# Four layers of cross attention and experts on one core: where the experts' downward sums are added up in six of ten passes

## The reference, cut to what matters

```python
mixed = jnp.zeros((T, D))
for e in range(E):                                   # E = 8
    mixed = mixed + flat_cw[:, e:e + 1] * _swiglu(flat_z, w1[e], w3[e], w2[e])
```

## Time and profile before

| what | value |
|---|---|
| median of three runs | 4637.65 us |
| the profiled execution's own time | 4653.02 us |
| its span, from first to last instruction | 4651.2 us |
| outside the span | 1.8 us |
| mean granted TensorE clock | 0.958 of full speed |
| busy TensorE / ScalarE / VectorE / GpSimd | 3977.9 / 3939.7 / 2817.9 / 830.5 us |

### The profile page before, as it was taken

One profiled execution on the slowest core, in us unless ns is written; L12 is line 12 of the kernel. 1 busy time (PEld: TensorE's weight loads), 2 busy tenths in 40 slices (PEclk: granted clock), 3 DMA queues, 4 the chain that ended last, 5 costly groups with the idle time before them and its releaser, 6 DMA issues. The chain is left out here.

```text
span 4651.2 us, 69670 instructions
## 1 busy us (share of the span) xinstructions
PE 3977.9 (86%) x26742; PEld 905.9 (19%) x26742; DVE 2817.9 (61%) x5645; ACT 3939.7 (85%) x4355; POOL 830.5 (18%) x719
## 2 busy tenths in 40 slices
PE   6888888888789888888989999888888888888887
PEld 2121111111122211122212222111111111122112
DVE  4878888778777788867501110110486668876833
ACT  3589998899888889888898889978988888888994
POOL 4010001520025200352412111111000210035002
PEclk7699999999999999999999999999999999999998
DMA  4221001100011100111102121110001100010001
GB/s 123 63 63 30 12 14 32 34 12 13 15 52 35 44 24 19 32 32 35 32 17 70 44 68 31 34 39 17 15 12 37 35 11 12 12 38 27 9 1 48
DMA packets 124358, 150.38 MB, mean 32 GB/s; under 512 B 29208, under 2 KB 76320, under 8 KB 124016
## 3 DMA queue, kind: packets, MB, share of 16 engines
q1 hardware_dynamic: 122576, 145.05, 11.6%
q10 hardware_dynamic: 1440, 0.79, 0.1%
HBM read 122.24 MB, written 23.51 MB: 31 GB/s over the span
## 5 line engine op out<-in xcount | busy, mean ns | idle before, releaser
L956 ACT ACTIVATE prob<-scores 128x1024 f32<-128x1024 f32 x3264 | 3177.7, 1025 | 314.2 <-PE scores L787 299.6
L1070 DVE TENSOR_REDUCE mpart<-side 128x1 f32<-128x512 f32 (+1 forms) x3456 | 2124.2, 657 | 729.8 <-PE side L818 719.1
L797 PE MATMUL av<-prob,VA 128*9 128x512 f32 x6528 | 875.0, 609 | 1.7 <-ACT prob L956 0.8
L797 PE MATMUL av<-prob,VB 128*9 128x512 f32 x6528 | 874.0, 608 | 1.3 <-ACT prob L956 0.5
L787 PE MATMUL scores<-QP,KA 32*128 32x512 f16 x3264 | 641.9, 395 | 195.1 <-ACT above L964 118.3
L787 PE MATMUL scores<-QP,KB 32*128 32x512 f16 x3264 | 631.3, 388 | 191.3 <-ACT above L964 93.7
L818 PE MATMUL side<-KA,QP 32*128 32x512 f16 (+1 forms) x2112 | 625.1, 392 | 39.6 <-DVE mpart L1070 20.7
L818 PE MATMUL side<-KB,QP 32*128 32x512 f16 (+1 forms) x2112 | 584.8, 386 | 43.2 <-DVE mpart L1070 29.2
L1074 DVE CUSTOM_DVE_ANT_0 above<-side,above 128x512 f32<-128x512 f32 x768 | 514.0, 686 | 76.0 <-PE side L818 70.0
L964 ACT ACTIVATE above<-scores 128x1024 f32<-128x1024 f32 x384 | 393.5, 1025 | 178.9 <-PE scores L809 116.1
L787 PEld LDWEIGHTS scores<-QP,KB 32*128 32x128 f16 x3264 | 151.8, 91 | 867.7 <-ACT prob L956 537.1
(11 more groups left out here) (185 smaller groups left out, 2541.5 us busy)
## 6 DMA issues: line engine op xcount, KB each, us to landing
cwb<-weights SPq DMA_DIRECT2D x80, 256.0 KB, 3.8
KA<-kstacks SPq DMA_DIRECT2D x384, 48.0 KB
KB<-kstacks SPq DMA_DIRECT2D x384, 48.0 KB
Fin<-in_Fin SPq DMA_DIRECT2D x64, 256.0 KB, 2.8
kstacks<-hi SPq DMA_DIRECT2D x112, 128.0 KB, 2.4
ctxc<-in_ctxT SPq DMA_DIRECT2D x48, 256.0 KB, 3.0
kstacks<-lo SPq DMA_DIRECT2D x56, 128.0 KB, 2.6
hT<-in_mask SPq DMA_DIRECT2D x16, 400.2 KB, 3.4
```

What stands on the lines that cost most here:

```text
L797: last = pe.matmul(AV[ROWS * h:ROWS * h + VC, :], V[l % 2][:, kt, g * HG + h, :], prob[:, (e + h // 2) % RING, (h % 2) * QB:(h % 2) * QB + ...
L956: act.activation(prob[:, e % RING, :], pair.rearrange("p a b -> p (a b)"), ACT.Exp if softmax(l) else ACT.Sigmoid, scale=SCALE).then_inc(s ...
L1070: dve.tensor_reduce(part, bank, AX.X, ALU.max).then_inc(sem["red"], 1)
```

## The change

In all passes VectorE's step `ysum` reads the downward bank and writes or adds `yT`. The step `yc`, GpSimd's step `ysum` and the buffer `yb` are gone. In the six passes where `by_dve` is false, `ysum` stands in the list directly behind the last downward matmul (gap 0); in the four others it keeps its gap of 3. The bank of a downward sum is free after `ysum` in all passes. `by_dve`, the gating and the copies of the upward matmuls stay as they are.

```diff
@@ last_use
     if what == "down":
-        return "ysum" if by_dve(*key[:2]) else "yc", key
+        return "ysum", key
@@ pass_steps
     def down(k, c):
         out.append((1, Step("PE", "down", (u, lp, k, c))))
         if c == n - 1:
-            if by_dve(u, lp):
-                out.append((3, Step("DVE", "ysum", (u, lp, k))))
-            else:
-                out.append((0, Step("ACT", "yc", (u, lp, k))))
-                out.append((0, Step("POOL", "ysum", (u, lp, k))))
+            out.append((3 if by_dve(u, lp) else 0, Step("DVE", "ysum", (u, lp, k))))
             if k + W_RING < E:
                 out.append((0, Step("SP", "wexp", (u, lp, k + W_RING))))
@@ build
-        yb = sb("yb", [P, 2, QB])
@@ scalar
-                elif s.what == "yc":
-                    u, lp, k = s.key
-                    own.wait_ge(*o.sem("down", u, lp, k, FFN[unit(u)[0]]["nk"] - 1))
-                    own.wait_ge(*o.sem("ysum", u, lp, k - 2))
-                    act.activation(yb[:, k % 2, :], bank_of(o, "down", u, lp, k), ACT.Copy).then_inc(sem["bgA"], 1)
@@ gpsimd
-                elif s.what == "ysum":
-                    u, lp, k = s.key
-                    own.wait_ge(*o.sem("yc", u, lp, k))
-                    if k == 0:
-                        own.wait_ge(*o.sem("cwput", u, lp))
-                        pool.tensor_copy(yT, yb[:, 0, :]).then_inc(sem["bgG"], 1)
-                    else:
-                        own.wait_ge(*o.sem("ysum", u, lp, k - 1))
-                        pool.tensor_tensor(yT, yT, yb[:, k % 2, :], ALU.add).then_inc(sem["bgG"], 1)
```

## The result

The changed kernel is slower: median 4653.42 us against 4642.16 us of the kernel before, 20 runs each. The ratio is 1.0024, with a 95 % interval from 1.0013 to 1.0035, some 11 us. I had forecast 5 us less, with a range of 4613 to 4653, within 0.5 %. The change is smaller than 0.5 %, to which I had given 0.83, but the sign is wrong and the median lies just outside the range. One run of the changed kernel took 5563 us with TensorE granted 0.635 of its clock; the comparison leaves it out.

A forecast was written before the change was run, and what follows sets the result against it. TensorE's background matmuls were taken to set much of the pace, with three engines briefly waiting for each other. Copies -11.1 and sums +5.8 gave -5.3 us: 4632 us against the 4637.65 median (profiled 4653.0 to 4648), range 4613 to 4653.

The forecast's parts named there:

- ScalarE's copies: 48 copies behind downward matmuls removed from ScalarE: 36 at 0.14, 9 at 0.48, 3 at 0.6 us, together 11.1 us gained.
- VectorE's sums: 48 added operations of 0.685 us behind downward matmuls, delaying search reductions; 0.12 us each passed on, 5.8 us lost, bounds 0 and 32.9.
- GpSimd's additions: 42 additions of 1.273 us removed from GpSimd, idle for four fifths of the span; costed at nothing.
- pacing: Planner counts `ysum` as VectorE work, 0.7 each, moving search tiles by a fraction of a beat; nothing, 3 us either side.
- ScalarE as the bound: Rival: ScalarE sets the end, so all of the copies and their waiting comes back, 38.7 us, 4599 us; chance 0.13.
- VectorE as the bound: Rival: sums delay reductions behind downward matmuls in search phases; 32.9 us less 11.1 gained, 22 us slower, 4660 us; chance 0.08.
- TensorE setting the beats alone: Rival: TensorE alone sets the beats where the change works, neither copies nor sums are seen, 4638 us; chance 0.20.
- a growth of ScalarE's waits for reductions by 15 us: Sign of being wrong towards slower: ScalarE's waits of `relu` for reductions, 44.8 us before, grow by 15 us or more.
- phases 3 and 30: Sign: these phases, which have no sums, should keep their lengths.
- phase 5: Sign: this phase, with six of the copies, should be shorter by under 2 us; losing 4 us means wrong towards faster.
- the exponential: Sign: ScalarE's exponential behind a downward matmul should start about 0.4 us after its end rather than 0.54.
- the reduction behind a downward matmul: Sign: the first VectorE reduction should start 0.76 us after the downward matmul's end rather than 0.40.

The follow-up runs named there:

- the list held fixed: Changed kernel with the planner's old reckoning, so every step but VectorE's sums stands where it stood before; ratio 0.9978 to the kernel before, median 4637.81 us.
- the tiny sums: Changed kernel with the sums of experts 1 to 6 in the six passes adding 8 columns, not 512; ratio 1.0027 to the kernel before, 4660.85 us.
- a second sum: Sums on VectorE with the planner's old reckoning, each of the 42 additions done twice, first into a spare buffer; ratio 1.0000 to the kernel before.
- by itself in the old kernel: Kernel before, copies and GpSimd's sums kept, its planner counting `ysum` on any engine; ratio 1.0035 to the kernel before, 4661.57 us against 4646.12.
- the two kernels with VectorE's sums: The changed kernel, and the same with the planner's old reckoning; ratios to the kernel before 1.0024 (again 1.0023) and 0.9978.
- the kernel in which the copy stays: Changed kernel, but ScalarE still copies to SBUF and VectorE adds from there, new reckoning; ratio 1.0070 to the kernel before, median 4681.51 us.

## Why the prediction was wrong, point by point

- **ScalarE's copies, -11.1 us, and VectorE's sums, +5.8 us, together -5.3.** With the list held fixed the two cost -10 us (-2 to -19 by the interval), and -4.2 us at equal clock. The sum was right in sign and about right in size. The sums' own term was over-sized: the tiny sums show nothing for 19 us of work, though in the changed kernel's list. What I took for pass-through, 0.12 us each, is nearer to what a second sum pays (0.2).
- **GpSimd's additions at nothing.** No run tests this alone. With the list fixed the whole move gained, so it cost nothing that can be seen.
- **"I cost it at nothing and keep 3 us to either side", of the pacing.** This is the step that failed. In its place the runs show 15 us by itself in the old kernel, and 21 us between the two kernels with VectorE's sums. I looked at the number of search tiles, which stays, and not at where they go. I did not ask which stalls stood near the places they left. The start of phases 12 and 28, where a small VectorE step waits for a load, was in the trace before: 1.15 us of waiting with 1.63 us of TensorE idle behind it.
- **The clock.** My prediction doesn't speak of it. The two kernels' mean granted clocks differ by 0.001 to 0.002, and each 0.001 is about 3 us. That is about half of the loss, if the clock is its cause. The sum had no term for a pause of TensorE that is followed by the lower clock, as the start of phase 28 shows one.
- **ScalarE as the bound** is refuted: with the list held fixed the move gave 10 us, by its interval at most 19, and not 38.7. The work taken from ScalarE was worth a quarter of that price.
- **VectorE as the bound** is refuted for the change: smaller sums gave nothing. With a second sum it begins to: 9 of the 29 us of added work are seen. The sign on which I would have called it, a growth of ScalarE's waits for reductions by 15 us, came in at 13.8, just under it, and had another cause.
- **TensorE setting the beats alone**, with neither copies nor sums seen, is hardly told apart from the forecast by the total with the list fixed, whose interval ends at -2 us. It holds for the phases at full clock to within 0.1 us for each sum: phases 5 and 9 are shorter by 0.6 and 0.7 us with six sums each.
- **The signs that I named** for phases 3 and 30 (unchanged), for phase 5 (shorter by under 2 us), for the exponential (0.37, forecast 0.4) and the reduction behind a downward matmul (0.65, forecast 0.76) came as written. The growth of the waits for scores (24.3 of 28.7) did too. ScalarE's busy time was to fall by 28.7 and VectorE's to rise by 33; they moved by 23.8 and 26.8, since I had not counted how records overlap. All these signs were local or sums over the whole span, and none of them could show a loss made by the planner.

## What to carry to other kernels

When an edit moves a step to an engine whose time a planner or a budget counts, write out the list before and after and see what else moved: here those moves were worth more than the edit, with the opposite sign. To judge an edit by itself, hold the rest of the list fixed. A step that waits for a load, a copy or anything of another engine should stand late in an in-order queue which others depend on, since those behind it wait too. Here that gave 12 us where the waits were long (2.4 to 2.8 us in phase 28) and nothing clear where they were short (1.2 to 1.5 us). A pause of TensorE can be paid a second time: in phase 28 the granted clock was at 0.50 for 6.8 to 13.7 us behind the long waits, and for 3.4 us or not at all behind the short ones.

## What was not expected of the hardware

- A run's time follows its mean granted TensorE clock closely: 3.0 to 3.3 us for 0.001 in most of the kernels here, with 1 to 3 us of scatter around the line. The spans of one kernel scatter by 5 to 9 us (standard deviation), so most of their scatter goes with the clock.
- TensorE's granted clock fell from 1.00 to 0.50 right behind a stretch of 4 us in which it was busy for 0.94 us, and stayed there for 13.7 us. In the first 15 us of the phase that it fell in, its mean was 0.75. The phase took 9.3 us longer, of which the longer wait for the load itself was 1.5 us (2.66 less 1.15).
- A VectorE operation with both inputs in SBUF was held up where a GpSimd operation had started up to 0.26 us before it. Of the sixteen of L1228 in the earlier trace rows, nine took 0.68 to 0.69 us and seven took 1.55 to 1.74, which makes the mean of 1.090. All seven started 0.08 to 0.26 us after GpSimd's L1367 had started and ended some 0.55 us after its end; the one that started 1.17 us after it and overlapped its last 0.10 us took 0.69. Two of the sixteen, and then GpSimd's operations beside them:

```profile
4621.30 0.69 DVE L1228 SCALAR_TENSOR_TENSOR ag<-tx,ag 128x512 f32<-128x512 f32 x1 [0.88 <-ACT ag L1006]
...
4623.20 1.55 DVE L1228 SCALAR_TENSOR_TENSOR ag<-tx,ag 128x512 f32<-128x512 f32 x1 [0.34 <-ACT ag L1006]
```

```profile
4619.91 1.27 POOL L1367 TENSOR_TENSOR hT<-hT,cwb 128x512 f32<-128x512 f32 x1 [1.50 <-DVE hT L1240]
4622.94 1.27 POOL L1367 TENSOR_TENSOR hT<-hT,cwb 128x512 f32<-128x512 f32 x1 [1.77 <-DVE hT L1240]
```

The one at 4621.30 had GpSimd idle beside it, the one at 4623.20 had not. Where GpSimd started second, at 4604.5, 0.17 us after VectorE, it was the one that took longer, 1.65 us in place of 1.27. The additions of the kernel in which the copy stays hardly met GpSimd, and took 0.694.
